# Picks in the rounded 4-byte float type with two parts, and 3.75 picked row tiles a step in layer 0

## What is computed

```python
# layer 0: a message for every edge, its maximum for every destination node
e = concat([x[src], x[dst], edge_attr])              # 3 x 32 features
v = relu(e @ W1 + b1) @ W2 + b2
x = layernorm(x + maximum(segment_max(v, dst), x))
# layer 1: relation-weighted messages with attention, their sum for every node
c   = w_comp[etype]
msg = einsum('eb,ebo->eo', c, einsum('ei,bio->ebo', h[src], weight))
a   = tanh(relu(sum(x_hat * y_hat) / sqrt(32)))      # x_hat of h[src]; y_hat of h[dst] and etype
h1  = relu(segment_sum(a * msg, dst) + h[src[last_e]] @ self_loop_weight)   # 0 without an edge
out = layernorm(h + h1)
```

## Time and profile before

| | us |
|---|---|
| median of the three runs | 5835.25 |
| span of the profiled execution, first to last instruction | 4310.2 |
| what lies around the span (the difference; no view shows it) | 1525.0 |
| GpSimd (POOL) busy in the span | 3192.4 |
| TensorE (PE) busy in the span | 3814.6 |
| VectorE (DVE) busy in the span | 3114.7 |

### The profile page before, as it was taken

How to read it: one execution, slowest core, us unless ns; L and a number is a source line. 1 busy time by engine, 2 the same in 40 slices (tenths; PEclk the granted TensorE clock), 3 DMA queues, 4 the chain that set the end, 5 groups by cost and what they waited for, 6 DMA issues and landing times.

```text
span 4310.2 us, 65460 instructions
## 1 busy us (share of the span) xinstructions
PE 3814.6 (89%) x23924; PEld 1783.4 (41%) x24179; DVE 3114.7 (72%) x5125; ACT 903.7 (21%) x1615; POOL 3192.4 (74%) x3330
## 2 busy tenths in 40 slices
PE   7989999999999999931989999999999999999941
PEld 3444554554545545411434434444434444434311
DVE  7856666666666666526688888888888888888844
ACT  4411111111111111110022222222222222222211
POOL 7777777777777777767777777777777777777745
PEclk9999999999999999975999999999999999999975
DMA  8123333333333333324145555555655555555611
GB/s 342 29 78 105 93 101 100 92 100 102 92 100 100 93 100 95 104 68 77 37 121 140 142 138 143 142 139 142 142 137 144 141 138 144 142 138 144 143 46 32
DMA packets 411502, 496.41 MB, mean 115 GB/s; under 512 B 165363, under 2 KB 314448, under 8 KB 409008
## 3 DMA queue, kind: packets, MB, share of 16 engines
q1 hardware_dynamic: 274800, 278.43, 25.0%
q0 software_dynamic: 106432, 131.97, 13.9%
q10 hardware_dynamic: 29952, 81.80, 5.2%
HBM read 345.09 MB, written 146.77 MB: 114 GB/s over the span
## 4 chain that ended last, share of the span: by engine, by line
DMA 22%; PE 16%; issue 9%; POOL 6%; DVE 3%; ACT 0%; POOLq 0%; DVEq 0%
DMA xg<-h_dram,src_idx 19%; POOL xg L699 6%; PE psum L1586 3%; PE psum L1519 3%; PE psum L1681 3%; PE psum L1510 3%; DMA last_rows<-sum_rows,last_i 2%; PE psum L1575 2%; DMA early<-max_rows,last_i 1%; PE psum L1411 1%; PE psum L1527 1%; DVE late L1256 0%; PE psum L1601 0%; PE psum L1572 0%; PE psum L1496 0%
## 5 line engine op out<-in xcount | busy, mean ns | idle before, releaser
L699 POOL DMA_INDIRECT xg<-h_dram,src_idx x1540 | 1475.4, 958 | 481.1 <-DMA xg<-h_dram,src_idx 345.7
L699 POOL DMA_INDIRECT xg<-in_x_dram,src_idx x1392 | 1329.8, 955 | 431.6 <-DMA xg<-in_x_dram,src_idx 305.3
L1256 DVE TENSOR_TENSOR late<-late,psum 128x512 f32<-128x512 f32 x1664 | 1078.1, 679 | 278.0 <-PE psum L1510 156.5
L1425 PE MATMUL psum<-early,late 128*128 128x448 bf16 x5712 | 1129.7, 353 | 9.7 <-DVE late L1054 7.6
L1425 PEld LDWEIGHTS psum<-early,late 128*128 128x128 bf16 x5712 | 544.6, 98 | 627.3 <-issue 113.9
L1510 PE MATMUL psum<-comp,sel 128*128 128x512 bf16 x1426 | 507.4, 384 | 18.5 <-DVE late L1256 14.3
L1519 PE MATMUL psum<-late,basis 128*32 128x512 f32 x3328 | 442.9, 604 | 12.8 <-issue 7.8
L1586 PE MATMUL psum<-x,late 128*128 128x448 bf16 x1344 | 380.6, 353 | 5.1 <-issue 5.1
L1054 DVE TENSOR_TENSOR late<-psum,lane_hot 128x448 f32<-128x448 f32 x272 | 169.8, 624 | 282.1 <-PE psum L1425 240.6
L1163 DVE TENSOR_TENSOR_SCAN scan<-fresh,scan,psum 128x512 f32<-128x512 bf16 x103 | 131.8, 1280 | 328.4 <-PE psum L1471 328.4
L1035 DVE TENSOR_SCALAR late<-late,class_id 128x384 bf16<-128x384 f32 (+2 forms) x728 | 336.6, 533 | 0.0
(11 more groups left out here) (159 smaller groups left out, 4394.4 us busy)
## 6 DMA issues: line engine op xcount, KB each, us to landing
sp_in<-spread SPq DMA_DIRECT2D x208, 256.0 KB, 3.8
late<-type_dram SPq DMA_DIRECT2D x104, 512.0 KB
sum_rows<-early ACTq DMA_DIRECT2D x104, 512.0 KB, 3.0
spread<-late SPq DMA_DIRECT2D x16, 1664.0 KB, 39.5
ea<-in_edge_t SPq DMA_DIRECT2D x104, 256.0 KB
keep<-keep_dram SPq DMA_DIRECT2D x832, 32.0 KB
max_rows<-out ACTq DMA_DIRECT2D x104, 256.0 KB
xg<-h_dram,src_idx POOLq DMA_INDIRECT x1540
```

What stands on the lines that cost most here:

```text
L699: pool.indirect_dma_start(out=out, out_offset=None, in_=table, in_offset=bass.IndirectOffsetOnAxis(ap=index, axis=0), engine_sem=pool_issu ...
L1256: dve.tensor_tensor(prod[:, n % G_BUFS, :], x4[:, s.slot(2), g, :], bank[C_BANK[n]][:, :], ALU.mult).then_inc(prod_ready, 1)
L1425: last_ = pe.matmul(hot_bank[tile_slot(s, t)], class_hot[s.slot(2)][:, HOT - hot_tiles(s) + t, c, :], x_parts[:, c, q, :], start=c == 0 an ...
```

## The change

- `x` and `h` are held as two parts in the rounded 4-byte float type (`float32r`), not as three bf16 parts. The one-hot matrices are in that type too, and so twice as large, in SBUF and in DRAM (448 KB a step saved and loaded). A picked tile takes 14 matmuls of 448 columns, not 21.
- Layer 0 picks 4, 4, 4 and 3 tiles in turn from step 8 on (steps 0 to 7 as before). `PIECES` gives where the three pieces end.
- The one-hot tiles of a step lie as [class][tile][128] and no more as [tile][class][128]: what one instruction of `build_hot` writes is one contiguous run.
- The split of `x` is 2 instructions a class, not 5, and waits in class 5 until two stores (`prep_out`) have landed; the split of `h` is 2 instructions a chunk, not 5.
- The step loops are unrolled as before; buffers are placed anew, and one wait (`hot_saved`) stands earlier.

```diff
+ROUNDED = 2
-HOT = 3
-HOTS = (2, 3, 3, 3)
+HOT = 4
+FIRST_HOTS = (2, 3, 3, 3)
+HOTS = (4, 4, 4, 3)
-PIECES = {1: (2, 4), 2: (5, 8), 3: (7, 12)}
+PIECES = {3: (7, 12), 4: (9, 16)}
-PICK_WORK = PARTS * CLASSES
+PICK_WORK = ROUNDED * CLASSES
...
-        hot_dram = dram("hot_dram", [STEPS * P, CLASSES * P], bf16)
+        hot_dram = dram("hot_dram", [STEPS * P, CLASSES * P])
...
+        class_hot = [rounded(f"class_hot{u}", [P, CLASSES, HOT, P], late_at + 4 * start)
+                     for u, start in enumerate((0, ZERO + ROW))]
+        x_parts = rounded("x_parts", [P, CLASSES, ROUNDED, PICK * F], early_at)
...
                 if n == 0:
+                    if c == CLASSES - 2:
+                        dve.wait_ge(prep_out, 32)
                     link(dve.tensor_copy(x_parts[:, c, 0, :], x_cls[:, c, :]))
-                elif n == 1:
-                    link(dve.tensor_tensor(x_rest[0], x_cls[:, c, :], x_parts[:, c, 0, :], ALU.subtract))
...
                 else:
-                    dve.tensor_copy(x_parts[:, c, 2, :], x_rest[1]).then_inc(parts_ready, 1)
+                    dve.tensor_tensor(x_parts[:, c, 1, :], x_cls[:, c, :], x_parts[:, c, 0, :], ALU.subtract
+                                      ).then_inc(parts_ready, 1)
...
                 for c in range(a, b):
-                    last_ = dve.tensor_scalar(class_hot[u][:, tiles, c, :], class_in[:, u, tiles, :],
+                    last_ = dve.tensor_scalar(class_hot[u][:, c, tiles, :], class_in[:, u, tiles, :],
                                               class_id[:, c:c + 1], None, ALU.is_equal)
...
-                    for q in range(PARTS):
+                    for q in range(ROUNDED):
                         last_ = pe.matmul(hot_bank[tile_slot(s, t)],
-                                          class_hot[s.slot(2)][:, HOT - hot_tiles(s) + t, c, :], x_parts[:, c, q, :],
-                                          start=c == 0 and q == 0, stop=c == CLASSES - 1 and q == PARTS - 1)
+                                          class_hot[s.slot(2)][:, c, HOT - hot_tiles(s) + t, :], x_parts[:, c, q, :],
+                                          start=c == 0 and q == 0, stop=c == CLASSES - 1 and q == ROUNDED - 1)
...
                 if pick:
-                    hot_rows(later, 0, 6)
+                    hot_rows(later, 0, 4)
...
-                    hot_rows(later, 6, 11)
+                    hot_rows(later, 4, 8)
...
-                    hot_rows(later, 11, 16)
+                    hot_rows(later, 8, 11)
...
-                    hot_rows(later, 16, 21)
+                    hot_rows(later, 11, 14)
```

More of the change, by code:

```diff
@@ L119, in hot_count @@
 def hot_count(n):
+    if n < PRE:
+        return FIRST_HOTS[n % len(FIRST_HOTS)]
     return HOTS[n % len(HOTS)] if n < FEW_HOT else 0
 def hot_tiles(s):
[L126 to L131 removed]
+    return hot_count(s.at)
 def tile_count(s, t):
[L136 to L138 removed]
+    return sum(hot_count(n) for n in range(s.at)) + t
 def tile_slot(s, t):
[L143 removed]
+    return tile_count(s, t) % 2
+FIRST_TILES = sum(hot_count(n) for n in range(PRE))
 def run_steps(eng, body, unroll, lead=1):
@@ L170, in dram, with rounded @@
             return nc.dram_tensor(name, shape, dt, kind="Internal").ap()
+        def rounded(name, shape, place):
+            return nc.alloc_sbuf_tensor_at(name, shape, f32r, offset=place)
         def sem(name):
@@ L312, in build @@
+        part(2 * CLASSES * P)
         early_picks = part(2 * PICK * F).rearrange("p (u h f) -> p u h f", u=2, h=PICK)
+        assert at[0] <= (2 * STREAMS + G_BUFS) * LEN
         at[0] = (2 * STREAMS + G_BUFS + 2 * STREAMS) * LEN
-        h_low = part(NODE_COLS * F // 2).bitcast(bf16).rearrange("p (c n) -> p c n", c=CLASSES)
-        hot1 = part(CLASSES * P).bitcast(bf16).rearrange("p (u c n) -> p u c n", u=2, c=CLASSES)
+        h_low = rounded("h_low", [P, CLASSES, PICK * F], late_at + 4 * at[0])
@@ L316, in build @@
+        part(NODE_COLS * F)
         picks1 = part(PICK * F).rearrange("p (h f) -> p h f", f=F)
-        h_high = x[:, :, :].rearrange("p t f -> p (t f)").bitcast(bf16).rearrange(
-            "p (c q n) -> p c q n", c=CLASSES, q=2)
-        h_parts = [h_high[:, :, 0, :], h_high[:, :, 1, :], h_low]
+        assert at[0] <= LATE
+        h_high = rounded("h_high", [P, CLASSES, PICK * F], x_at)
+        h_parts = [h_high, h_low]
+        assert CLASSES * P <= 2 * LEN and CLASSES * P <= 2 * SLOTS * F
@@ L321, in build @@
+        hot1 = [rounded(f"hot1_{u}", [P, CLASSES, P], place) for u, place in enumerate((ea_at, out0_at))]
         x_cls = x[:, :, :].rearrange("p (c k) f -> p c (k f)", c=CLASSES)
@@ L453, in gathered0 @@
         def gathered0(s, use):
-            hots = HOTS[s.slot(PRE) % len(HOTS)]
-            return s.earlier(PRE) * 16 * (SLOTS - hots) + use * 16 * (SLOTS - hot_tiles(s))
+            past = sum(SLOTS - hot_count(n) for n in range(s.slot(PRE), s.at, PRE))
+            return 16 * (past + use * (SLOTS - hot_tiles(s)))
         def hot(s):
@@ L628, in _ @@
             border_rows(sp, max_rows, 0)
+            for u in range(2):
+                sp.wait_ge(hot_saved[u], 16 * (STEPS // 2))
             early_v = early_dram.rearrange("(q n) -> q n", n=TILES * P)
```

62 lines of the change are left out of this document (28 added, 34 removed).

## The result

| | runs | median, us | lowest to highest |
|---|---|---|---|
| before | 4 | 5835.11 | 5824.73 to 5839.68 |
| after | 4 | 5911.81 | 5899.38 to 5929.50 |

The ratio is 1.0118, 95% interval 1.0093 to 1.0143. Forecast were 5740 us and a range of 5708 to 5800. The profiled run of after took 5911.4 us.

The account below looks back on a forecast made before the run. POOL's stream of gathers and scatters was taken as the bound, TensorE just behind. Layer 0 gains 89 us and layer 1 6 us: 5835.25 - 95 = 5740 us, range 5708 to 5800.

Parts of the forecast that it names:

- what lies around it (1525.0 us) stays: Whole run: the time outside the profiled span of 4310.2 us was taken as unchanged, giving 5740 us.
- GpSimd's stream is the clock: Whole span: POOL's gathers and scatters set the pace, one gather every 1.251 us in layer 0, 1.268 in layer 1.
- the bank waits: Layer 0, fourth tile: TensorE waits for VectorE to read a PSUM bank, 0.2 us in 68 steps, 13.6 us.
- One pass for the new type, the load hidden: Picked matmuls: 0.42 ns a column, 0.1896 us each as in bf16, with the weight load costing nothing.
- rival A: Picked matmuls: the new type takes two cycles a column, 0.38 us a matmul, about 6680 us in all; chance 0.13.
- My sum for TensorE alone: Layer 0: TensorE's own path, with 4788 matmuls at 0.1896 us, ends at 1796 us, 9 us before POOL's.
- the forecast of 95 us: Whole span: a gain of 89 us in layer 0 and 6 us in layer 1.
- A gather is worth 1.251 us: Layer 0: each gather saved shortens POOL's path by 1.251 us, so 92 fewer give 115.1 us.
- The stretch: Layer 0: VectorE's fast builds lengthen POOL's gathers by 0.3 us a step, 27 us over 91 steps.
- Rival C: Layer 0: an exclusive port lock makes all seven builds block POOL, 2.8 us a step, 5970 us in all; chance 0.02.
- The start: Layer 0, before step 8: POOL's idle gap of 5.81 us goes, pacing gives some 5 back, net gain 1 us.
- Layer 1: Layer 1: POOL sets the pace; only its wait for the coefficients can be gained, 6 us.

Follow-up runs that it names:

- the one with a single part: After, but layer 1 picks h with its first part alone, 7 matmuls a step in place of 14: 1.0100 times before, beside after at 1.0147.
- the three-tile kernel: After with three picked tiles a step in layer 0 and seven more products a step in layer 1, their sum thrown away: 4287.74 us against before's 4308.73.

## Why the prediction was wrong

**The step that failed** is the last one: "what lies around it (1525.0 us) stays: 5835.25 - 95 = 5740 us". A span of 4310 us beside runs of 5835 us was not a program with 1525 us around it. It was an execution at the fast pace, and the timed runs were at the slow one, in which something else is the bound: before's own span is 5911.1 us in a run of 5912.9. Everything I read from the profile held for the fast pace alone. The warning stood in the two numbers, and I named the gap without asking what could fill it. No rival covered it.

**"GpSimd's stream is the clock"** is true at the fast pace and false at the slow one. There GpSimd starts 1190 gathers in 1900 us of layer 0 in before and 1108 in after on the same chip. By the chain that ended last (TensorE 42%, unnamed releasers 28%, VectorE 15%) a step is bound by the handshakes between TensorE and VectorE, with completions that lag. So 92 gathers fewer are worth nothing: after takes 30 us more than the kernel with the same type and the old tiles, and against before its layer 0 ends 9 us earlier in the one pair of profiles, not 115. TensorE's part of that chain did not shrink: 342 x 14 products at a median of 206 ns are 986 us, 250 x 21 at 189 ns were 992. That this is why layer 0 gains so little is argued and not shown: with three tiles the products shrink to 273 x 14 x 0.206 = 787 us and layer 0's last gather comes at 2374 us, with the old tiles to 250 x 14 x 0.206 = 721 us, and it comes at 2377, both within the range of after's profiles.

**The loss** has two parts. The smaller is the fourth tile: three tiles instead of 3.75 take 44 us off after, and 15 us off the kernel with bf16 in layer 1; which of its costs this is (the products, the bank waits, the longer builds) stays open. The larger is layer 1's: 1.3 us less work on TensorE a step, which I had as a gain of 6 us. At the slow pace this term has the wrong sign: layer 1's gathers took 44 to 63 us longer in the profiles of after than in the one of before. Shown: bf16 picks there, or seven more products, each take 64 us off; bytes don't. Only argued: that the granted clock does it. Its share fits four kernels, but not the one with a single part. Why less work makes layer 1 longer stays open. So does the size of the loss: it was 64 to 85 us where before took 5835 to 5853 us, and 31 to 41 us where before took 5908 to 5919.

**By the other steps, at the fast pace:**

- *One pass for the new type, the load hidden.* Nearly. 206 ns from start to start (median, with loads of 191 ns under them), not 189.6; rival A's 380 ns falls. But 4788 matmuls at 0.206 are 986 us, not 908. My sum for TensorE alone becomes 281.2 + 54.6 + 484.1 + 986.3 + 54.6 + 13.6 = 1874, above the 1802 of GpSimd. And the median flatters: 7% of the picked matmuls of the three-tile kernel at the fast pace are some 300 ns apart and 2% at 373 ns, the lower clock, and the mean is 0.216 us, past the 0.213 from which TensorE ends no earlier than before. So even at the fast pace the forecast of 95 us was too high: by this estimate layer 0 gains nothing (by the mean) to 1894 - 1874 = 20 us (by the median) and layer 1 10 to 15 us, 10 to 35 us in all. After was never met at the fast pace; this stays an estimate.
- *A gather is worth 1.251 us.* Held at the fast pace: there the three-tile kernel has 23 gathers fewer, worth 28.8 us, and its last gather of layer 0 moved by 28 us, from 1891 to 1863. The two items below, 6.5 us gained and 7.6 lost, nearly cancel.
- *The stretch.* Right in size for four tiles, too large for three. A build of three tiles takes 2.38 us (0.34 an instruction), and with three tiles in every step the mean distance of layer 0's gathers at the fast pace went from 1.2510 to 1.2570 us: 0.08 us a step. A build of four tiles takes 2.86 us (0.41 an instruction), and the mean gather from `x` lasts 980 ns in after against 954 in before at the slow pace and 957 with three tiles; in the loop of layer 0, which is all but the first gathers, some 25 ns more on 12.25 gathers a step make 0.3 us, as forecast. Rival C (2.8 us a step) falls.

```profile
1504.83 2.86 DVE L1043 TENSOR_SCALAR class_hot<-late,class_id 128x512 fp32r<-128x512 f32 x7
L710 POOL DMA_INDIRECT xg<-in_x_dram,src_idx x1300 | 1273.7, 980 | 910.8 <-DMA src_idx<-in_src_t 308.7
L699 POOL DMA_INDIRECT xg<-in_x_dram,src_idx x1392 | 1328.4, 954 | 906.6 <-issue 319.1
```

- *The start.* GpSimd's first gather of step 8 comes at 276.6, not 283.1: 6.5 us gained, not 1.
- *Layer 1.* From first to last gather 1945 us with 14 products of the new type, 1960 with bf16: 15 us gained in this pair of profiles (the medians of the two kernels are 9.5 us apart), not 6. With seven products more it is 1959: the gain was TensorE's.

## What to carry to other kernels

Before any sum, set the profiled execution's span against the timed runs. Here the two are 2 us apart wherever both are of one execution; a gap of 1525 us meant that the profile was of another execution and told nothing of the bound in those that were timed. A relief of an engine is only worth what the chain behind it lets through; at the slow pace it was even a loss. Where completions lag, count the round trips between engines, not the busy time.

## What the runs showed of the hardware

- The same kernel on the same chip was met at 4309 and at 5915 us, and at 4311 and 5919 us on another. At the slow pace events of TensorE's semaphores come 6 to 10 us (medians in before, at a step's end) behind the matmul's recorded end, in bunches. The cause is open. The Trainium skill (NOTIFIC — the notification-queue block, 7.1 Overflow: three behaviours, one of which stalls the engine) says that when a queue of records is full the block drops new records, overwrites old ones or, in its third mode, stalls their producer. What fits it here: of before's 98,699 semaphore events at the fast pace 39,547 are left at the slow one, most of the missing ones of DMAs, while all 65,460 instructions are there; in the layers that is 5 to 7 events a us, not 24. No run here tells it from another cause, or says whether the kernel would be slow if nothing were recorded: every timed run of the experiments came with a recorded span.
- More work on TensorE can make a kernel faster: seven products a step without use, 64 us of 5950.
- A matmul with 4-byte rounded operands and 448 columns costs 206 ns (median) from start to start at the upper clock, against 189 for bf16, while its weight load lasts 191 to 200 ns (means) against 98. A full f32 product of 512 columns took 0.86 us.
- VectorE's builds of 128x512 into the 4-byte rounded type go with longer gathers: in layer 0's loop a gather lasts 0.947 us on average in before and 0.970 to 0.975 in the seven profiles of after, but 0.952 with builds of 128x384. In the kernel that also writes bf16 matrices between those builds it is 0.949.

```profile
L1431 PEld LDWEIGHTS psum<-x_parts,class_hot 128*128 128x128 f32 x5096 | 992.1, 200 | 483.6 <-issue 256.6
```
